# Two graph convolutions of a four-layer GNN kernel: the product with the weights, the scaling by degrees and the split into bf16 parts gathered into one stage

## The chip, the cores and the metric

One core of one Trainium2 chip runs the whole kernel. The metric is the device time of one execution in microseconds (us); the kernel before takes 8021.73 us, the median of three runs.

## What is computed

Four graph layers follow each other, each added to its input and normalised over 64 features. The change touches the last one, two graph convolutions over 6250 nodes:

```python
def _gcn_conv(x, src, dst, W, b):
    h = x @ W
    deg = 1.0 + jax.ops.segment_sum(jnp.ones_like(dst, dtype=h.dtype), dst, num_segments=N)
    dinv = jax.lax.rsqrt(deg)
    norm = dinv[src] * dinv[dst]
    msg = h[src] * norm[:, None]
    agg = jax.ops.segment_sum(msg, dst, num_segments=N)
    return agg + h * (1.0 / deg)[:, None] + b
h = jax.nn.relu(_gcn_conv(x, src, dst, W1, b1))
return _gcn_conv(h, src, dst, W2, b2)
```

There are 200000 edges. `x` is 6250 x 64 and `W` 64 x 64, all f32.

## The kernel before, in words

The nodes stand as 125 partitions by 50 blocks (NL = 125, NB = 50) by 64 features (D). Earlier stages have sorted the edges and made `counts`, a matrix of u8 edge counts between nodes, in tiles of 128 x 128; a row of it is 50 such tiles, 800 KB, loaded as two halves of 400 KB. Edges that found no slot there are "spilled" and handled one by one.

A convolution is two stages, each a block of its own with a rendezvous of all engines at its end.

`project` (line 517, called in lines 2100 and 2102) computes x @ W in f32, two blocks a round, 25 rounds. ScalarE copies a block to a buffer (L539), TensorE transposes ("turns") it (L553), ScalarE copies the turned block out of PSUM (L544), TensorE multiplies it with the weights (L557, which the profile shows as two instructions for one f32 product), VectorE copies the product to `hh` (L565, in the profile `node_sums`). There are two buffers of everything.

`convolve` (line 1990) calls `spread` (from line 1306) with one pass. On VectorE it begins with `before_vector`: `xs = h * dinv` for all 3200 elements of a partition (L1996), then `to_parts` (L1140 to L1143), which splits `xs` into three bf16 parts whose sum is the f32 value: cast, subtract, cast, subtract. A wait for a constant (`spilled.const`) stands ahead. Then come the 50 rows of `counts`. SyncE loads the tiles (L1338, two rows ahead), ScalarE (L1374) and VectorE (L1458) each cast their share of a tile to bf16, TensorE multiplies 50 tiles with the parts (L1395) and adds the node's own row (L1403), VectorE sums the three parts' columns (L1464), and later, two rows at a time, finishes `z` (L2001 to L2009). TensorE handles the first two rows together and finishes both at the end. A row's cast buffer is free again when TensorE has finished the row two before.

The spilled edges run beside. GpSimd clears `y_rows` at the start (L1200). ScalarE, in its queue behind its four first casts and a wait on `posted`, which VectorE raises after `before_vector`, writes `xs` to a table in memory, `rows` (L1193). GpSimd waits for that table, reads the spilled edges (L1208), and gathers their nodes (L1216); after row 5 TensorE compares ids (L1236), VectorE scales the gathered rows (L1269), TensorE sums (L1242), GpSimd adds the result to `y_rows` (L1222) and loads it as `y_sb` (L1227). TensorE and VectorE stand in their queues at this point until that work is through; rows 6 and on come after it.

The stage that opens the whole kernel (`front`) has turns in groups of four blocks (L143) and products with 192 columns (L132), its copies all on VectorE; the sort stage has f32 products of 64 columns (L402). The last layer norm (L1102 to L1111) follows the second convolution.

Of the kernel before, what the change touches and what calls it, by code (L numbers as in the profile page):

```python
# [5 lines left out]
F32, BF16, I32, I16, U8 = mybir.dt.float32, mybir.dt.bfloat16, mybir.dt.int32, mybir.dt.int16, mybir.dt.uint8  # L6
ALU, ACT, AX = mybir.AluOpType, mybir.ActivationFunctionType, mybir.AxisListType

N_NODES, D = 6250, 64
N_EDGES = 200000  # L10
NB = 50
NL = N_NODES // NB
# [499 lines left out]
                dve.tensor_copy(n_spilled[:], pad_f[:, 0:1])  # L512
                dve.tensor_copy(n_pairs[:], pad_f[:, 1:2])

def project(nc, tag, x, weights, out, ident, n_out):

    with ExitStack() as ctx:
        sb = lambda name, shape, dt: ctx.enter_context(nc.sbuf_tensor(f"{tag}_{name}", shape, dt))  # L520
        pb = lambda name, shape: ctx.enter_context(nc.psum_tensor(f"{tag}_{name}", shape, F32))
        sem = ctx.enter_context(Semaphores(nc))
        two = range(2)
        block = [sb(f"block{u}", [NL, D], F32) for u in two]
        block_t = [sb(f"block_t{u}", [D, NL], F32) for u in two]
        ps_t = [pb(f"ps_t{u}", [128, 512]) for u in two]
        ps_o = [pb(f"ps_o{u}", [128, 512]) for u in two]
        taken = sem("taken")

        staged, turned, turned_sb, product, kept = (sem(n) for n in ("staged", "turned", "turned_sb", "product", "kept"))  # L530
        with nc.Block() as blk:
            @blk.scalar
            def _(act):
                act.sem_inc(turned, 2)
                act.sem_inc(product, 2)
                with act.Fori(0, NB // 2) as it:
                    for u in two:
                        act.wait_ge(turned, 2 * it + (u + 1))
                        act.activation(block[u][:], x[:, bass.ds(2 * it + u, 1), :].rearrange("p a d -> p (a d)"),  # L539
                                       ACT.Copy).then_inc(staged, 1)  # L540
                    for u in two:
                        act.wait_ge(turned, 2 * it + (u + 3))
                        act.wait_ge(product, 2 * it + (u + 1))
                        act.activation(block_t[u][:], ps_t[u][0:D, 0:NL], ACT.Copy).then_inc(turned_sb, 1)  # L544

            @blk.tensor
            def _(pe):
                pe.sem_inc(kept, 2)
                with pe.Fori(0, NB // 2) as it:
                    for u in two:  # L550
                        pe.wait_ge(staged, 2 * it + (u + 1))
                        pe.sem_inc(taken, 1)
                        nc.tensor.transpose(ps_t[u][0:D, 0:NL], block[u][:], ident[0:NL, 0:NL]).then_inc(turned, 1)  # L553
                    for u in two:
                        pe.wait_ge(turned_sb, 2 * it + (u + 1))
                        pe.wait_ge(kept, 2 * it + (u + 1))
                        nc.tensor.matmul(ps_o[u][0:NL, 0:n_out], block_t[u][:], weights, start=True,  # L557
                                         stop=True).then_inc(product, 1)

            @blk.vector  # L560
            def _(dve):
                with dve.Fori(0, NB // 2) as it:
                    for u in two:
                        dve.wait_ge(product, 2 * it + (u + 3))
                        dve.tensor_copy(out[:, bass.ds(2 * it + u, 1), :].rearrange("p a d -> p (a d)"),  # L565
                                        ps_o[u][0:NL, 0:n_out]).then_inc(kept, 1)


N_RP = NB // 2
# [568 lines left out]
def to_parts(link, dve, parts, whole, rest):  # L1138

    link(dve.tensor_copy(parts[:, :, 0, :], whole[:]))  # L1140
    link(dve.tensor_tensor(rest[:], whole[:], parts[:, :, 0, :], ALU.subtract))
    link(dve.tensor_copy(parts[:, :, 1, :], rest[:]))
    link(dve.tensor_tensor(parts[:, :, 2, :], rest[:], parts[:, :, 1, :], ALU.subtract))  # L1143


def wide(col):

    return col[:].unsqueeze(2).to_broadcast([NL, NB, D])
# [130 lines left out]
def pair_rows(p):  # L1279
    return slice(2 * p, 2 * p + 2) if isinstance(p, int) else bass.ds(2 * p, 2)  # L1280
# [706 lines left out]
               lambda k: 2 if k == PASSES - 1 else 7, False)  # L1987


def convolve(nc, tag, shared, ident16, h, out, bias, relu, dinv, xs, parts, sums, y_sb, rest, counts):  # L1990

    with ExitStack() as ctx:
        z = ctx.enter_context(nc.sbuf_tensor(f"{tag}_z", [NL, 2, D], F32))

        def before_vector(dve, link):
            link(dve.tensor_tensor(xs[:], h[:], wide(dinv), ALU.mult))  # L1996
            to_parts(link, dve, parts, xs, rest)

        def post(dve, link, k, p):
            b = pair_rows(p)  # L2000
            link(dve.tensor_tensor(z[:], sums[:, b, :], y_sb[:, b, :], ALU.add))  # L2001
            yield
            link(dve.tensor_tensor(z[:], z[:], dinv[:, b].unsqueeze(2).to_broadcast([NL, 2, D]), ALU.mult))
            yield
            link(dve.tensor_tensor(z[:] if relu else out[:, b, :], z[:],
                                   bias[:].unsqueeze(1).to_broadcast([NL, 2, D]), ALU.add))
            yield
            if relu:
                link(dve.tensor_scalar(out[:, b, :], z[:], 0.0, None, ALU.max))  # L2009
                yield  # L2010

        spread(nc, tag, 1, counts, SRC, DST, *shared, ident16, xs, (parts, parts), sums, y_sb, before_vector, post,
               lambda k: 4 if relu else 3, True)


def load_layer3(nc, io, w, bias):
    with ExitStack() as ctx:
        loaded = ctx.enter_context(Semaphores(nc))("w3_loaded")
        with nc.Block() as blk:
            @blk.sync  # L2020
            def _(sp):
                for i in range(2):
                    sp.dma_start(w[i][:], io[f"L3_gnn_W{i + 1}"]).then_inc(loaded, 16)
                    sp.dma_start(bias[i][:], io[f"L3_gnn_b{i + 1}"].rearrange("(a n) -> a n", a=1)
                                 .to_broadcast([NL, D])).then_inc(loaded, 16)
                sp.wait_ge(loaded, 64)


def build(nc, io, out):
# [7 lines left out]
    counts = dram("counts", [NB, 128, NB, 128], U8)  # L2037
    counts_t = dram("counts_t", [NB, 128, NB, 128], U8)
    Semaphores.made = {}
    with ExitStack() as ctx:  # L2040
        sb = lambda name, shape, dt, c=ctx: c.enter_context(nc.sbuf_tensor(name, shape, dt))
        n_spilled = sb("n_spilled", [TE, 1], I32)
        n_pairs = sb("n_pairs", [TE, 1], I32)
        x = sb("x", [NL, NB, D], F32)
        ident = sb("ident", [128, 128], F32)
        ident16 = sb("ident16", [128, 128], BF16)
# [23 lines left out]
        hh = node_sums[:, :, 0:D]  # L2070
        xs, y_sb = [sb(name, [NL, NB, D], F32) for name in ("xs", "y_sb")]

        both = sb("sums_rest", [NL, 2, NB, D], F32)
        sums, rest = both[:, 0], both[:, 1]
        parts2 = both[:].rearrange("p a b d -> p (a b d)").bitcast(BF16)[:, 0:NB * 3 * D]\
            .rearrange("p (b i d) -> p b i d", i=3, d=D)
        parts = sb("parts", [NL, NB, 3, D], BF16)
        dinv1, dis2, dinv3 = (sb(name, [NL, NB], F32) for name in ("dinv1", "dis2", "dinv3"))
        coeff = sb("coeff", [NL, 6], F32)
        w3 = [sb(f"w3_{i}", [D, D], F32) for i in range(2)]  # L2080
        bias3 = [sb(f"bias3_{i}", [NL, D], F32) for i in range(2)]
        rows = dram("rows", [N_NODES, D], F32)
        y_rows = dram("y_rows", [NL * YB, D], F32)
        shared = (io, sorted_rows, rows, y_rows, n_pairs, ident)
# [12 lines left out]
        layer_norm(nc, "ln2", x, hh[:], 1.0, rest)  # L2097

        load_layer3(nc, io, w3, bias3)
        project(nc, "conv1_of", x, w3[0][:], hh, ident, D)  # L2100
        convolve(nc, "conv1", shared, ident16, hh, hh, bias3[0], True, dinv3, xs, parts, sums, y_sb, rest, counts)
        project(nc, "conv2_of", hh, w3[1][:], hh, ident, D)
        convolve(nc, "conv2", shared, ident16, hh, hh, bias3[1], False, dinv3, xs, parts, sums, y_sb, rest, counts)
        layer_norm(nc, "ln3", x, hh[:], 1.0, rest, out_rows=out)


# [24 lines left out]
```

## Time and profile before

| what | value |
|---|---|
| time, median of 3 runs | 8021.73 us (8019.52 to 8025.28) |
| time of the profiled execution | 8040.06 us |
| its span | 8038.4 us |
| TensorE matmul busy | 6943.2 us (86%) |
| VectorE busy | 5984.2 us (74%) |
| ScalarE busy | 4364.3 us (54%) |
| the two projections | 7401 to 7447, 7701 to 7747 us |
| the two stages with the matrix rows | 7448 to 7699, 7747 to 7998 us |
| last layer norm | from 8001 us |

The profile comes from one execution, the times of which lie some 18 us above the median. Busy times are averages over very different stages; what the change touches is read from the timeline of its own stretches. PE is TensorE, PEld its weight loads, DVE VectorE, ACT ScalarE, POOL GpSimd, SP SyncE; a trailing q is the engine's queue issuing a DMA. The number behind x counts the instructions that a row merges, and the bracket tells how long the engine was idle before and what ended that.

### The profile page before, as it was taken

The numbers are of one execution on the slowest core, as the hardware profiler recorded it, in microseconds if no ns is written. First come the engines' busy times: TensorE is split into PE (matmuls) and PEld (weight loads), VectorE is DVE, ScalarE is ACT, GpSimd is POOL, SyncE is SP. The second block draws the span as 40 slices with busy tenths as digits, with TensorE's granted clock in tenths as the row PEclk, the third lists the DMA queues.
The fourth block names the chain that finished last, engine by engine and source line by source line (L and its number), as shares of the span: only waits on it lengthen the run. The fifth ranks groups of instructions, "written<-read, shape, count | busy, mean of one in ns | idle before, by whom it ended". The sixth has DMA issues, their size and how long they took to land. (4 is left out here: it accounts for less than half of the span.)

```text
span 8038.4 us, 279490 instructions
## 1 busy us (share of the span) xinstructions
PE 6943.2 (86%) x98699; PEld 5917.8 (74%) x98724; DVE 5984.2 (74%) x17395; ACT 4364.3 (54%) x13164; POOL 2862.3 (36%) x2957
## 2 busy tenths in 40 slices
PE   2499999999999799999994788888895999998887
PEld 1255555555555499999993787787895988897877
DVE  4367677767776699898995799799898766775556
ACT  0122222222222299999993787787794655665545
POOL 0388888888888755454552000000000000000000
PEclk9999999999999999999996999999998999998878
DMA  7622222322222277676674887787894766664645
GB/s 309 226 59 59 61 59 59 60 60 59 60 60 59 53 233 232 223 233 227 229 231 139 287 298 275 280 300 275 297 334 178 200 197 197 198 195 122 182 132 153
DMA packets 656412, 1425.60 MB, mean 177 GB/s; under 512 B 284336, under 2 KB 351662, under 8 KB 652737
## 3 DMA queue, kind: packets, MB, share of 16 engines
q1 hardware_dynamic: 542402, 1245.12, 48.0%
q0 software_dynamic: 101792, 92.82, 5.5%
q10 hardware_dynamic: 11668, 80.52, 2.5%
q8 instruction: 322, 5.28, 0.3%
q14 instruction: 228, 1.87, 0.1%
HBM read 982.95 MB, written 433.34 MB: 176 GB/s over the span
## 5 line engine op out<-in xcount | busy, mean ns | idle before, releaser
L330 POOL DMA_INDIRECT sorted_rows<-sort_rows,sort_row_at x1600 | 1979.6, 1237 | 579.7 <-issue 566.6
L1593 ACT ACTIVATE smooth_msg<-smooth_ps_a,smooth_w_rows 128x64 f32<-128x64 f32 x6000 | 1312.4, 333 | 335.4 <-PE smooth_ps_a L1679 317.5
L360 ACT ACTIVATE sort_count<-sort_ps_c 50x50 bf16<-50x50 f32 x1600 | 331.7, 207 | 1935.7 <-PE sort_ps_c L392 1935.7
L1374 ACT ACTIVATE poly_cast<-poly_mat 128x1536 bf16<-128x1536 uint8 x500 | 713.9, 1475 | 462.1 <-PE poly_ps L1395 359.0
L388 PEld LDWEIGHTS sort_ps_r<-sort_count,sort_hot_dt 50*125 50x125 bf16 x1600 | 283.0, 177 | 837.3 <-issue 582.8
L402 PE MATMUL sort_ps_m<-sort_w,sort_hidden 128*125 128x64 f32 x3200 | 879.3, 430 | 0.0
L381 PE MATMUL sort_ps_h<-sort_attrs,sort_w 24*128 24x500 f32 x800 | 812.0, 1116 | 45.1 <-DMA sort_attrs<-in_attr_t 45.1
L1701 PE MATMUL smooth_ps_s<-smooth_msg,smooth_hot 128*128 128x64 bf16 x7500 | 771.3, 195 | 82.3 <-DVE smooth_last_part L1832 66.1
L1701 PE MATMUL smooth_ps_s<-smooth_rest,smooth_hot 128*128 128x64 bf16 x7500 | 766.8, 194 | 6.5 <-issue 6.5
L1701 PE MATMUL smooth_ps_s<-smooth_last_part,smooth_hot 128*128 128x64 bf16 x7500 | 765.9, 194 | 6.9 <-issue 6.9
L402 PEld LDWEIGHTS sort_ps_m<-sort_w,sort_hidden 128*125 128x125 f32 x3200 | 732.1, 320 | 41.1
L1701 PEld LDWEIGHTS smooth_ps_s<-smooth_msg,smooth_hot 128*128 128x128 bf16 x7500 | 687.5, 99 | 99.8 <-DVE smooth_last_part L1832 67.9
L741 ACT ACTIVATE graph_hot_t<-graph_ps_t 128x1024 bf16<-128x1024 bf16 x625 | 641.7, 1027 | 126.9 <-PE graph_ps_t L784 96.6
L1701 PEld LDWEIGHTS smooth_ps_s<-smooth_rest,smooth_hot 128*128 128x128 bf16 x7500 | 690.3, 99 | 15.4 <-issue 15.4
L1701 PEld LDWEIGHTS smooth_ps_s<-smooth_last_part,smooth_hot 128*128 128x128 bf16 x7500 | 687.4, 98 | 11.3 <-issue 11.2
L1395 PE MATMUL poly_ps<-parts,poly_cast 125*128 125x192 bf16 x7500 | 643.4, 250 | 55.1 <-DVE poly_cast L1458 24.1
L817 PE MATMUL graph_ps_kv<-kv_parts,graph_hot_t 125*128 125x128 bf16 x7500 | 686.1, 219 | 0.0
L1822 DVE TENSOR_TENSOR smooth_rest<-smooth_msg 128x640 f32<-128x640 f32 x750 | 617.8, 824 | 88.1 <-ACT smooth_msg L1593 34.4
L1395 PEld LDWEIGHTS poly_ps<-parts,poly_cast 125*128 125x128 bf16 x7500 | 633.1, 99 | 65.2 <-issue 28.0
L711 POOL TENSOR_TENSOR graph_parts<-graph_parts 128x260 f32<-128x260 f32 x625 | 387.4, 620 | 745.2 <-DVE graph_hot L873 740.7
L814 PE MATMUL graph_ps_q<-q_parts,graph_hot_t 125*128 (+1 forms) x7500 | 633.0, 193 | 15.5 <-ACT graph_hot_t L741 9.2
L1832 DVE TENSOR_TENSOR smooth_last_part<-smooth_rest 128x640 bf16<-128x640 f32 x750 | 616.0, 821 | 13.8
(332 smaller groups left out, 16537.9 us busy)
## 6 DMA issues: line engine op xcount, KB each, us to landing
poly_mat<-counts_t SPq DMA_DIRECT2D x500, 400.0 KB, 3.7
smooth_src<-src_rows SPq DMA_DIRECT2D x150, 960.0 KB, 5.1
smooth_hot<-hot_rows SPq DMA_DIRECT2D x150, 960.0 KB, 7.0
smooth_src<-src_rows SPq DMA_DIRECT2D x150, 640.0 KB, 5.9
smooth_hot<-hot_rows SPq DMA_DIRECT2D x150, 640.0 KB, 7.0
graph_edges<-sorted_rows SPq DMA_DIRECT2D x125, 700.0 KB
hot_rows<-graph_hot SPq DMA_DIRECT2D x125, 640.0 KB, 3.6
src_rows<-graph_hot_t SPq DMA_DIRECT2D x125, 640.0 KB, 3.5
```

The lines of the kernel that those rows point to most:

```text
L330: pool.indirect_dma_start(out=sorted_rows, out_offset=bass.IndirectOffsetOnAxis(row_at[u][:, j:j + 1], 0), in_=rows[u][:, j, :], in_offset ...
L381: nc.tensor.matmul(ps_h[h][:, 0:H * TE], w1[:], attrs[u][:, h * H * TE:(h + 1) * H * TE], start=True, stop=True).then_inc(hidden_ps, 1)
L402: last = nc.tensor.matmul(ps_m[u][0:TE, t * D:(t + 1) * D], hidden[u][:, t * TE:(t + 1) * TE], w2[:], start=True, stop=True, skip_group_ch ...
L741: act.activation(hot_t[x.b][:, :, :, x.s, :].rearrange("p e t v d -> p e t (v d)"), ps_t[x.g % 2][:].rearrange("p e t v d -> p e t (v d)") ...
L814: nc.tensor.matmul(ps_q[:, 2 * t + v], d_t, q[:, i], start=i == 0, stop=i == 2, skip_group_check=True)
L817: last = nc.tensor.matmul(ps_kv[u][:, 2 * t + v], s_t, kv_parts[:, s, i], start=i == 0, stop=i == 2, skip_group_check=True)
L1374: act.activation(cast[u][h][:, DVE_S:HR, :], mat[u][h][:, DVE_S:HR, :], ACT.Copy)\
L1395: last = nc.tensor.matmul(ps[u][:, 0:3 * D], cast[u][b // HR][0:NL, b % HR, :], parts[k % 2][:, b].rearrange("p i d -> p (i d)"), start=b ...
L1593: last = act.activation(at[:, i, :], ps_a[g % 2][:, i * D:(i + 1) * D], ACT.Copy, scale=w_rows[u][:, c * CHUNK + i:c * CHUNK + i + 1])
L1701: last = nc.tensor.matmul(ps_s[u][:, 0:D], hot[u][t][:, at // 2, :, at % 2], part[:, i, :], start=False, stop=c == N_CHUNKS - 1 and i == C ...
L1822: dve.tensor_tensor(rest[c][:], msg[c][:], high(msg[c]), ALU.subtract).then_inc(firsts, 1)
L1832: dve.tensor_tensor(last_part[c][:], rest[c][:], high(rest[c]), ALU.subtract)\
```

## The change

`project` is gone. A new stage, `conv_rows`, takes a block's rows directly from `x` for the turn, with no copy ahead. It turns four blocks into one PSUM bank and copies them with one ScalarE instruction, multiplies each with the weights into a bank that holds eight blocks, scales eight blocks by `dinv` with one VectorE instruction straight from PSUM into `xs`, and makes the three parts there too, eight blocks at a time: the two casts on ScalarE, the two subtractions on VectorE. TensorE turns group i before it multiplies group i-1. `before_vector` is empty, and `hh` no longer holds the product.

```diff
-def project(nc, tag, x, weights, out, ident, n_out):
...
-def convolve(nc, tag, shared, ident16, h, out, bias, relu, dinv, xs, parts, sums, y_sb, rest, counts):
+def conv_rows(nc, tag, x, w, dinv, xs, parts, left, ident):
...
+            @blk.tensor
+            def _(pe):
+                def products(i):
+                    pe.wait_ge(turned_sb, i + 1)
+                    o = quads[i].start // OCT
+                    if o >= 2 and quads[i].start == octs[o].start:
+                        pe.wait_ge(scaled, o - 1)
+                    for b in range(quads[i].start, quads[i].stop):
+                        at = b - octs[o].start
+                        last = nc.tensor.matmul(ps_o[o % 2][0:NL, at * D:(at + 1) * D],
+                                                xt[i % 2][:, (b - quads[i].start) * NL:(b - quads[i].start + 1) * NL], w,
+                                                start=True, stop=True, skip_group_check=True)
+                    if quads[i].stop == octs[o].stop:
+                        last.then_inc(product, 1)
+
+                for i, q in enumerate(quads):
+                    if i >= 2:
+                        pe.wait_ge(turned_sb, i - 1)
+                    for b in range(q.start, q.stop):
+                        last = nc.tensor.transpose(ps_t[i % 2][0:D, (b - q.start) * NL:(b - q.start + 1) * NL], x[:, b, :],
+                                                   ident[0:NL, 0:NL])
+                    last.then_inc(turned, 1)
+                    if i >= 1:
+                        products(i - 1)
+                products(len(quads) - 1)
+
+            @blk.scalar
+            def _(act):
+                def turn(i):
+
+                    act.wait_ge(turned, i + 1)
+                    act.activation(xt[i % 2][:, 0:size(quads[i]) * NL], ps_t[i % 2][0:D, 0:size(quads[i]) * NL], ACT.Copy)\
+                       .then_inc(turned_sb, 1)
+
+                def first(o):
+                    act.wait_ge(scaled, o + 1)
+                    act.activation(parts[:, octs[o], 0, :], xs[:, octs[o], :], ACT.Copy).then_inc(firsts, 1)
+
+                def second(o):
+                    act.wait_ge(rests, o + 1)
+                    act.activation(parts[:, octs[o], 1, :], left[:, octs[o], :], ACT.Copy).then_inc(seconds, 1)
+
+                n = len(octs)
+                for i in range(n + 3):
+                    for j in (2 * i, 2 * i + 1):
+                        if j < len(quads):
+                            turn(j)
+                    if 0 <= i - 2 < n:
+                        first(i - 2)
+                    if 0 <= i - 3 < n:
+                        second(i - 3)
+
+            @blk.vector
+            def _(dve):
+                def scale(o):
+                    dve.wait_ge(product, o + 1)
+                    s = octs[o]
+                    dve.tensor_tensor(xs[:, s, :], ps_o[o % 2][0:NL, 0:size(s) * D].rearrange("p (b d) -> p b d", d=D),
+                                      dinv[:, s].unsqueeze(2).to_broadcast([NL, size(s), D]), ALU.mult).then_inc(scaled, 1)
+
+                def rest(o):
+                    dve.wait_ge(firsts, o + 1)
+                    dve.tensor_tensor(left[:, octs[o], :], xs[:, octs[o], :], parts[:, octs[o], 0, :], ALU.subtract)\
+                       .then_inc(rests, 1)
+
+                def last_part(o):
+                    dve.wait_ge(seconds, o + 1)
+                    dve.tensor_tensor(parts[:, octs[o], 2, :], left[:, octs[o], :], parts[:, octs[o], 1, :], ALU.subtract)
+
+                n = len(octs)
+                for o in range(n + 2):
+                    if o < n:
+                        scale(o)
+                    if 1 <= o <= n:
+                        rest(o - 1)
+                    if o >= 2:
+                        last_part(o - 2)
+
+
+def convolve(nc, tag, shared, ident16, out, bias, relu, dinv, xs, parts, sums, y_sb, counts):
...
         def before_vector(dve, link):
-            link(dve.tensor_tensor(xs[:], h[:], wide(dinv), ALU.mult))
-            to_parts(link, dve, parts, xs, rest)
+            pass
...
-        project(nc, "conv1_of", x, w3[0][:], hh, ident, D)
...
+        conv_rows(nc, "conv1_of", x, w3[0][:], dinv3, xs, parts, rest, ident)
...
```

With NB = 50 there are 13 groups of four blocks (`quads`, the last of two) and 7 of eight (`octs`, the last of two). The second convolution is changed in the same way.

## Rows read from the trace of the kernel before

**Rows 1.** Busy time by stretch, first projection (columns named in the first line)

```profile
core 0: us, PE busy (x) PEld busy (x) DVE busy (x) ACT busy (x) POOL busy (x), PEclk, DMA share, GB/s
7401.00:7447.00 46.00, 41.38 (x150) 27.31 (x150) 11.11 (x50) 23.09 (x100) 0.00 (x0) 0.50 0.00 0
```

**Rows 2.** Timeline of the first projection: start, length, engine, line, operands

```profile
7401.29 0.45 ACT L539 ACTIVATE conv_of_block<-x 125x64 f32 x2 [11.86 <-ACTq L534]
...
7443.87 1.10 PE L557 MATMUL conv_of_ps_o<-w,conv_of_block_t 64*125 64x64 f32 x4
...
7444.90 0.62 PE L553 MATMUL conv_of_ps_t<-ident,conv_of_block 125*64 125x125 f32 x2
...
7446.92 0.23 DVE L565 COPY node_sums<-conv_of_ps_o 125x64 f32 x1 [0.20 <-PE conv_of_ps_o L557]
```

**Rows 3.** Timeline of the first convolution's entry to its matrix rows

```profile
7448.40 0.27 SPq L1188 DMA_DIRECT2D conv_before<-in_tri  x1
...
7450.30 1.32 POOL L1200 DMA_DIRECT2D y_rows<-conv_zeros  x1 [0.30 <-POOL conv_zeros L1198]
7450.97 3.49 DVE L1996 TENSOR_TENSOR xs<-node_sums,dinv 125x3200 f32<-125x3200 f32 x1 [3.83 <-DMA conv_lane_col<-in_lanes]
7452.98 5.86 ACT L1374 ACTIVATE conv_cast<-conv_mat 128x1536 bf16<-128x1536 uint8 x4 [7.15 <-DMA conv_mat<-counts]
...
7465.33 0.26 ACTq L1193 DMA_DIRECT2D rows<-xs  x1
...
7466.51 10.02 PE L1395 MATMUL conv_ps<-parts,conv_cast 125*128 125x192 bf16 x98 [19.75 <-DVE conv_cast L1458]
```

**Rows 4.** Timeline of the opening stage, four turns and the products after them

```profile
72.37 1.04 PE L143 MATMUL front_ps_t<-ident,x 125*64 125x125 f32 x4
...
73.34 2.92 PE L132 MATMUL front_ps_o<-w_qkv,front_xt 64*125 64x192 f32 x8
```

**Rows 5.** The sort stage: a stretch (columns as rows 1), four f32 instructions in it

```profile
2000.00:2006.00 6.00, 5.41 (x19) 3.10 (x19) 3.83 (x16) 2.22 (x7) 4.78 (x5) 1.00 0.26 62
...
2004.94 1.10 PE L402 MATMUL sort_ps_m<-sort_w,sort_hidden 128*125 128x64 f32 x4
```

**Rows 6.** Groups of instructions of three other sizes (count, busy us, mean ns, idle before)

```profile
L544 ACT ACTIVATE conv_of_block_t<-conv_of_ps_t 64x125 f32<-64x125 f32 x100 | 24.1, 270 | 36.4 <-PE conv_of_ps_t L553 36.4
...
L741 ACT ACTIVATE graph_hot_t<-graph_ps_t 128x1024 bf16<-128x1024 bf16 x625 | 641.7, 1027 | 126.9 <-PE graph_ps_t L784 96.6
...
L1822 DVE TENSOR_TENSOR smooth_rest<-smooth_msg 128x640 f32<-128x640 f32 x750 | 617.8, 824 | 88.1 <-ACT smooth_msg L1593 34.4
```

**Rows 7.** Timeline of the first convolution, from row 1's end past the spilled edges

```profile
7476.62 0.25 PE L1403 MATMUL conv_ps<-parts,ident 125*128 125x192 bf16 x1
...
7482.25 4.23 ACT L1374 ACTIVATE conv_cast<-conv_mat 128x1536 bf16<-128x1536 uint8 x3 [3.64 <-DMA conv_mat<-counts]
...
7482.94 1.19 POOL L1208 DMA_DIRECT2D conv_edges<-sorted_rows  x1 [31.33 <-DMA rows<-xs]
...
7490.67 1.22 POOL L1216 DMA_INDIRECT conv_of_node<-rows,conv_from_at  x1 [0.30 <-issue]
...
7500.22 0.62 PE L1236 MATMUL conv_ps_spill<-ident,conv_edges 125*125 125x125 f32 x4
...
7504.42 0.29 DVE L1269 TENSOR_TENSOR conv_msg<-conv_of_node,conv_edges 125x128 f32<-125x128 f32 x1
...
7505.71 6.93 PE L1395 MATMUL conv_ps<-parts,conv_cast 125*128 125x192 bf16 x50
...
7512.57 4.29 PE L1395 MATMUL conv_ps<-parts,conv_cast 125*128 125x192 bf16 x50
```

**Rows 8.** Transfers: two stretches (columns as rows 1), two issues of 7447:7520

```profile
7458.00:7461.00 3.00, 0.00 (x0) 0.00 (x0) 2.97 (x2) 0.84 (x1) 0.00 (x0) 0.50 0.32 133
...
7467.00:7470.00 3.00, 3.00 (x21) 2.75 (x20) 2.22 (x3) 0.00 (x0) 0.00 (x0) 0.50 0.93 309
...
y_rows<-conv_zeros POOLq DMA_DIRECT2D x1, 1593.8 KB, 18.9
...
conv_of_node<-rows,conv_from_at POOLq DMA_INDIRECT x2, 4.4
```

More of the change, by code:

```diff
@@ L513, in _ @@
                 dve.tensor_copy(n_pairs[:], pad_f[:, 1:2])
-def project(nc, tag, x, weights, out, ident, n_out):
[L519 to L566, printed above, removed]
@@ L1987, in polynomial @@
                lambda k: 2 if k == PASSES - 1 else 7, False)
-def convolve(nc, tag, shared, ident16, h, out, bias, relu, dinv, xs, parts, sums, y_sb, rest, counts):
+def conv_rows(nc, tag, x, w, dinv, xs, parts, left, ident):
+    QUAD, OCT = 4, 8
+    with ExitStack() as ctx:
+        sb = lambda name, shape, dt: ctx.enter_context(nc.sbuf_tensor(f"{tag}_{name}", shape, dt))
+        pb = lambda name, shape: ctx.enter_context(nc.psum_tensor(f"{tag}_{name}", shape, F32))
+        sem = ctx.enter_context(Semaphores(nc))
+        two = range(2)
+        xt = [sb(f"xt{u}", [D, QUAD * NL], F32) for u in two]
+        ps_t = [pb(f"ps_t{u}", [128, 512]) for u in two]
+        ps_o = [pb(f"ps_o{u}", [128, 512]) for u in two]
+        turned, turned_sb, product, scaled, firsts, rests, seconds = (
+            sem(n) for n in ("turned", "turned_sb", "product", "xs_scaled", "firsts", "rests", "seconds"))
+        quads = [slice(b, min(b + QUAD, NB)) for b in range(0, NB, QUAD)]
+        octs = [slice(b, min(b + OCT, NB)) for b in range(0, NB, OCT)]
+        size = lambda s: s.stop - s.start
+        with nc.Block() as blk:
+            @blk.tensor
[65 more added lines that the diff above has]
+                        last_part(o - 2)
@@ L2099, in build @@
         load_layer3(nc, io, w3, bias3)
-        project(nc, "conv1_of", x, w3[0][:], hh, ident, D)
-        convolve(nc, "conv1", shared, ident16, hh, hh, bias3[0], True, dinv3, xs, parts, sums, y_sb, rest, counts)
-        project(nc, "conv2_of", hh, w3[1][:], hh, ident, D)
-        convolve(nc, "conv2", shared, ident16, hh, hh, bias3[1], False, dinv3, xs, parts, sums, y_sb, rest, counts)
+        conv_rows(nc, "conv1_of", x, w3[0][:], dinv3, xs, parts, rest, ident)
+        convolve(nc, "conv1", shared, ident16, hh, bias3[0], True, dinv3, xs, parts, sums, y_sb, counts)
+        conv_rows(nc, "conv2_of", hh, w3[1][:], dinv3, xs, parts, rest, ident)
+        convolve(nc, "conv2", shared, ident16, hh, bias3[1], False, dinv3, xs, parts, sums, y_sb, counts)
         layer_norm(nc, "ln3", x, hh[:], 1.0, rest, out_rows=out)
```

## The prediction

> **What bounds the kernel now.** I read the page's first part (TensorE 86% busy, but that is an average over stages), then the busy time by stretch around the places that the diff touches, then their timelines. Everything changed lies after 7395 us, in two like copies, one for each convolution.
>
> In the projection, 46 us long, TensorE counts as busy for 41.4 us at a granted clock of 0.50 (the 1.2 GHz level), ScalarE for 23 us, VectorE for 11 us [rows 1]; the second projection is its twin. The timeline shows why this busy TensorE is not a full one: 25 rounds of two blocks take the 45.9 us from ScalarE's first copy at 7401.29 to the end of VectorE's last at 7447.15, 1.8 each, and only 1.03 of that passes between the start of two blocks' products (7443.87) and the next turns (7444.90); the rest goes round over ScalarE's copies [rows 2]. It is a chain of handovers, not an engine at its limit.
>
> Then comes a stretch in which TensorE does nothing. The block is entered at 7448.40 (called B). VectorE waits to B+2.57 for a small constant, then scales and splits in five wide instructions until 7465.3, and only then casts its share of the first matrix rows; TensorE starts at 7466.51, B+18.1, though ScalarE has been casting since 7452.98. The table that the spilled edges are gathered from is written behind VectorE's work too, at 7465.33, B+16.9 [rows 3]. All of this lies on the path.
>
> **Part 1, the stage.** Removed per convolution: 100 ScalarE copies, 50 VectorE copies and the five wide VectorE instructions. TensorE keeps its 50 turns and 50 products, in 13 and 7 groups. Added: 13 wide copies and 14 casts on ScalarE, 21 instructions on VectorE. No DMA is added.
>
> TensorE: the opening stage has the same groups of four turns; from the first to the product behind them it is 73.34 - 72.37 = 0.97 us [rows 4]. Two blocks' products (each shows as two instructions) take 7444.90 - 7443.87 = 1.03 us to the next work, and VectorE's copies behind single products come 0.43 us apart (0.23 long, 0.20 idle), so 0.21 for one instruction more: four blocks are 1.03 + 4 x 0.21 = 1.87 [rows 2]. A group of four is 2.84 us; 12 of them and a half one (0.55 + 1.03) make 35.7 us.
>
> Does the clock change that? In the sort stage, at a granted clock of 1.00, four such instructions with 64 columns take 1.10 us, as four do here at 0.50 [rows 2, 5]. So I put nothing down for the clock.
>
> ScalarE: 125 columns take 270 ns, 1024 take 1027 ns [rows 6], so 0.84 ns a column: 0.59 us for a group's turns, 0.60 for a part of eight blocks. Per eight blocks 2.4 us beside TensorE's 5.7: hidden. VectorE: 3200 columns take 3.49 us [rows 3], 640 take 0.82 [rows 6], 1.04 ns each, so 0.69 us for 512 and about 0.29 for the last 128; three of 0.69 are 2.1 us: hidden. At the end the cover is gone: behind the product group before the last, which ends 1.0 us before TensorE does, VectorE's queue holds six instructions of 0.69 and three of 0.29, 5.0 us, plus some 0.4 of handovers. The stage ends at 7401.3 + 35.7 - 1.0 + 0.1 + 5.4 = 7441.5 in place of 7447.15: **gain 5.6 us**. Bounds: all 150 instructions at 0.21 with no cost of switching, 31.5 us, gain 9.8; products at the opening stage's 2.92 a group (192 columns there) [rows 4], 12.5 x 1.05 = 13 us more, a loss of 7.5.
>
> **Part 2, the start of the block.** `before_vector` is empty now. ScalarE's first cast starts at B+4.6 and takes 1.48, VectorE's first can run beside it, so TensorE starts near B+6.1 in place of B+18.1 [rows 3]. What is late next?
>
> Rows 0 and 1 take 10.1 us as before (7466.51 to 7476.62) [rows 3, 7]: B+16.3. With two rows of buffers, row 2 is cast only then: 1.9 us for a cast and its handovers, then 4.3 a row [rows 3, 7], so B+22.5, row 3 B+26.8. Tiles now travel beside two long transfers. The clearing of y_rows alone moves 133 GB/s at a share of 0.32, about 5 of 16 engines [rows 8]. The table lands 17.6 us after its issue (7482.94, when GpSimd reads the edges) and ScalarE waits 3.6 us for a tile that comes at 7482.25 [rows 3, 7]. In the new kernel the table is issued behind ScalarE's four casts, at B+10.5, and lands near B+28.1; with slow tiles until then, row 4 ends near B+31, row 5 near B+36.
>
> After row 5 the spilled edges are due. The second gather is issued 7.7 us after the table's landing and lands 4.4 later [rows 7, 8]: new B+40.2. VectorE's own steps need 4.2 us from TensorE's arrival (7500.22 to 7504.42) [rows 7]: B+40.2. The rows go on 1.3 us later (7505.71) [rows 7]: B+41.5 in place of B+57.3, 15.8 us. 1.8 of it I keep back: TensorE idles before the spill, and behind such an idle the next row took 6.9 us where 4.3 is usual [rows 7]. **Gain 14 us.** Bounds: 16.5 if the table lands in 15 us; 7, below.
>
> **Sum.** 19.6 a convolution, 39 us. Behind the spill nothing differs: same rows, same reload of y_sb, same layer norm. The profiled execution took 8040.06 us (span 8038.4), 18 above the median of 8021.73; the terms are differences, so they come off the median: **7983 us**.
>
> **Rivals.**
> 1. TensorE has no cost of switching: 2 x (9.8 + 14) = 48, 7974; with the table in 15 us 7969. For: both helpers have slack. Against: four turns and the switch take 0.97 us, not 4 x 0.21 [rows 4]. Chance 0.17.
> 2. The clearing and the table share engines. The clearing lands 18.9 us after 7450.30, B+20.8 [rows 3, 8]; today it meets the table for 3 us, then for 10. Sharing puts the table up to 7 or 8 us later, and the spill with it: part 2 gains 7, time 8021.7 - 25 = 7997. For: 0.32 is 5 engines, and the table has the same 125 partitions. Against: when both ran, with tiles, the share was 0.93 [rows 8]. Chance 0.17. The Trainium skill ("DMA: Bandwidth & Descriptors", "Why a DMA increments its semaphore by 16 and not by 1") takes the largest number up to 16 that divides the outer size, 5 for 125, which the 0.32 bears out; by it ScalarE's transfers use the lowest-numbered engines and GpSimd's a run from a moving cursor, so that an overlap hangs on the cursor. The time would be this rival's.
> 3. Lock step, the slower one: ScalarE and VectorE wait in fixed orders. If a part's wait stood before the next turn, TensorE would wait round the ring: per eight blocks 5.7 + 1.2 + 2.1 + 1.2 = 10.2 us, 64 us a stage against my 40.2. 24 worse, 19.6 better: 8030, and 8056 with products at 2.92 a group. It decides once a helper's queue needs over 5.7 us per eight blocks. Against: `first(i-2)` stands behind turns 2i and 2i+1, what it waits for is two groups old. Chance 0.03.
> 4. The casts don't start early (something else holds VectorE or the tiles): 8021.7 - 11 = 8011. Chance 0.04.
> 5. The fuller stage brings TensorE its 2.4 GHz level, and f32 work halves: TensorE 18 us, gain 23 a stage, 2 x (23 + 14): 7948. Against: four instructions take 1.10 us at either level [rows 2, 5]. Chance 0.02. The Trainium skill ("TensorE: Matmul & The Clock Gate", "What's actually happening") has the array at half its clock when cold, and its gaps are columns over clock; the trace does not bear that out for these f32 products.
>
> The forecast has 0.57, its own range 7977 to 7991; with most of rivals 1 and 2 the range is **7970 to 7999**. A measurement of this kernel tells about 0.2%, 16 us, from no change. Faster by more: 0.57 + 0.17 + 0.17 + 0.02 = 0.93; within: 0.05 (rival 4, the milder half of 3); slower: 0.02.
>
> **What would show it.** About 40 us from the first turn to VectorE's end, groups of four turns 2.84 us apart; TensorE's first matrix product at B+6; the table issued at B+10.5; the spill's message product at B+40; the rows after it at B+42. Wrong would be: groups over 3.5 us apart, ScalarE waiting for VectorE inside the stage, or the rows going on later than B+50.

## The result, and the profile after

The changed kernel took 8005.68 us, the median of 13 executions. Twelve of them lie from 7985.19 to 8012.01; the other, a slow one at 8364.18, was left out of the comparison. The kernel before, run beside it, took 8028.91 us (8019.52 to 8038.58). The two medians are 23 us apart; the ratio over the executions that were kept is 0.9966, 95% interval 0.9958 to 0.9974: about 27 us, 0.34% faster, and this is the figure that I use. I had forecast 39 us and 7983. The kernel before ran 7 us above the 8021.73 from which I had counted, so part of the distance to 7983 is that; 12 us of gain are missing all the same.

| us | before | after |
|---|---|---|
| profiled execution, its span | 8038.4 | 7986.8 |
| start of the layer norm ahead of the convolutions | 7371.1 | 7357.2 |
| from there to B, the first convolution's block | 77.3 | 69.8 |
| from B to the second convolution's B | 298.9 | 280.2 |
| from there to the end | 291.1 | 279.7 |

The first line differs by 51.6 us, which is not the change's worth: 14 of it lie ahead of all that the diff touches. In five profiled executions of the two kernels (two of the one, three of the other) that start lies at 7371.1 and 7362.8 us, and at 7357.2, 7359.4 and 7360.1; in the nine profiled variants below, which leave this stretch alone, anywhere from 7359.3 to 7368.7. The last three lines of the table, the **last part** from here on, add up to 667.3 and 629.7; over the five executions they are 667.3 and 663.3 before, 629.7, 635.6 and 629.3 after, means 665.3 and 631.5, **33.8 us** apart. That is what the change can be seen to do in the profiles. The timed 27 lies some 7 below it, and these 7 I can't place. The three profiled executions of the changed kernel took 7988.53, 7996.67 and 7991.07 us; seven of the twelve above took 8004 to 8012, and no profile shows one of those, so what they do otherwise is open.

The page of the changed kernel, its first lines:

```profile
span 7986.8 us, 278076 instructions
## 1 busy us (share of the span) xinstructions
PE 6915.9 (87%) x98699; PEld 5905.6 (74%) x98724; DVE 5887.1 (74%) x17327; ACT 4339.6 (54%) x13018; POOL 2861.7 (36%) x2957
```

Busy time says little of where the time went: TensorE's fell from 6943.2 to 6915.9, VectorE's from 5984.2 to 5887.1.

The stage, by stretch (answers to [rows 1]):

```profile
core 0: us, PE busy (x) PEld busy (x) DVE busy (x) ACT busy (x) POOL busy (x), PEclk, DMA share, GB/s
7386.00:7427.00 41.00, 35.38 (x150) 28.68 (x150) 12.33 (x21) 14.49 (x27) 0.00 (x0) 0.50 0.00 1
```

TensorE is busy from its first turn to its last product without a gap (35.38 us from 7386.76 to 7422.14), and the granted clock is 0.50 throughout, the 1.2 GHz level. Its timeline, and VectorE's tail (answers to [rows 2]):

```profile
7386.76 1.85 PE L1975 MATMUL conv_of_ps_t<-ident,x 125*64 125x125 f32 x8 [33.60 <-PEq L48]
...
7390.40 1.04 PE L1975 MATMUL conv_of_ps_t<-ident,x 125*64 125x125 f32 x4
...
7391.37 1.94 PE L1965 MATMUL conv_of_ps_o<-w,conv_of_xt 64*125 64x64 f32 x8
...
7419.36 2.78 PE L1965 MATMUL conv_of_ps_o<-w,conv_of_xt 64*125 64x64 f32 x12
...
7421.33 0.69 DVE L2013 TENSOR_TENSOR xs<-conv_of_ps_o,dinv 125x512 f32<-125x512 f32 x1 [1.87 <-PE conv_of_ps_o L1965]
...
7424.74 0.89 DVE L2023 TENSOR_TENSOR parts<-sums_rest,parts 125x512 bf16<-125x512 f32 x2
```

Four turns (7390.40), then the products of the group before (7391.37), and the next turns at 7393.24: a group takes 2.84 us. All ScalarE and VectorE work hides behind it until 7421.33. L2013 scales, L2018 subtracts, L2023 makes the last part.

The entry (answers to [rows 3]); B is 7426.93:

```profile
7426.93 0.27 SPq L1136 DMA_DIRECT2D conv_before<-in_tri  x1
...
7428.82 1.32 POOL L1148 DMA_DIRECT2D y_rows<-conv_zeros  x1 [0.30 <-POOL conv_zeros L1146]
7430.80 2.86 ACT L1322 ACTIVATE conv_cast<-conv_mat 128x1536 bf16<-128x1536 uint8 x2 [5.62 <-DMA conv_mat<-counts]
7430.80 2.10 DVE L1406 CAST conv_cast<-conv_mat 128x1664 bf16<-128x1664 uint8 x2 [5.16 <-DMA conv_mat<-counts]
...
7432.34 4.02 PE L1343 MATMUL conv_ps<-parts,conv_cast 125*128 125x192 bf16 x24 [10.20 <-ACT conv_cast L1322]
```

VectorE now casts its share at once, and TensorE starts at B+5.4 in place of B+18.1. ScalarE and GpSimd further on (answers to [rows 7]):

```profile
7434.37 1.48 ACT L1322 ACTIVATE conv_cast<-conv_mat 128x1536 bf16<-128x1536 uint8 x1 [0.71 <-DMA conv_mat<-counts]
7435.39 0.26 ACTq L1141 DMA_DIRECT2D rows<-xs  x1
...
7442.84 2.86 ACT L1322 ACTIVATE conv_cast<-conv_mat 128x1536 bf16<-128x1536 uint8 x2 [5.62 <-PE conv_ps L1351]
7447.14 1.48 ACT L1322 ACTIVATE conv_cast<-conv_mat 128x1536 bf16<-128x1536 uint8 x1 [1.44 <-DMA conv_mat<-counts]
7455.08 4.23 ACT L1322 ACTIVATE conv_cast<-conv_mat 128x1536 bf16<-128x1536 uint8 x3 [6.46 <-DMA conv_mat<-counts]
...
7456.20 1.68 POOL L1156 DMA_DIRECT2D conv_edges<-sorted_rows  x1 [26.07 <-DMA rows<-xs]
...
7464.71 1.22 POOL L1164 DMA_INDIRECT conv_of_node<-rows,conv_from_at  x1 [0.30 <-issue]
...
7469.05 0.62 PE L1184 MATMUL conv_ps_spill<-ident,conv_edges 125*125 125x125 f32 x4
...
7473.24 0.29 DVE L1217 TENSOR_TENSOR conv_msg<-conv_of_node,conv_edges 125x128 f32<-125x128 f32 x1
```

The fifth of these lines is the one that matters: ScalarE idles 6.46 us until 7455.08, B+28.2, and what ends it is a tile of counts, the second of row 3. TensorE stands still before it:

```profile
7452.00:7455.00 3.00, 0.00 (x0) 0.00 (x0) 0.00 (x0) 0.00 (x0) 0.00 (x0) 0.78 0.52 179
```

Here no engine works at all: the kernel waits for a transfer. The transfers issued in 7426 to 7500 (answers to [rows 8]):

```profile
conv_mat<-counts SPq DMA_DIRECT2D x28, 400.0 KB, 4.9
y_rows<-conv_zeros POOLq DMA_DIRECT2D x1, 1593.8 KB, 24.9
```

The clearing of `y_rows` takes 24.9 us from issue to landing, 18.9 before; the table, issued at B+8.5, lands at B+29.3 (7456.20): 20.8 us, 17.6 before.

### The profile page after: what moved, and what is told of

Read it like the earlier page. It is cut to its first block and busy times, and to the rows that moved or that the text cites. A ratio compares the mean times of both kernels' runs of the same rounds, so it can differ in the third digit from the quotient of the medians.

```text
span 7986.8 us, 278076 instructions
## 1 busy us (share of the span) xinstructions
PE 6915.9 (87%) x98699; PEld 5905.6 (74%) x98724; DVE 5887.1 (74%) x17327; ACT 4339.6 (54%) x13018; POOL 2861.7 (36%) x2957
## 3 DMA queue, kind: packets, MB, share of 16 engines
q14 instruction: 229, 1.88, 0.1%
## 5 line engine op out<-in xcount | busy, mean ns | idle before, releaser
L402 PEld LDWEIGHTS sort_ps_m<-sort_w,sort_hidden 128*125 128x125 f32 x3200 | 732.3, 320 | 41.1
```

The source lines that it names most:

```text
L402: last = nc.tensor.matmul(ps_m[u][0:TE, t * D:(t + 1) * D], hidden[u][:, t * TE:(t + 1) * TE], w2[:], start=True, stop=True, skip_group_ch ...
```

## The experiments

All were run beside the kernel before, whose medians in the four sets were 8029.7, 8027.01, 8028.26 (one run) and 8030.56 us. Ratios are to these.

**Both kernels again.** No edit.

> The kernel before, unchanged. Measures what repeats. In the first profile the part from the start of the third layer norm to the end took 667.2 us (8038.4 - 7371.1). Theory A (the change's own part is steady, the untouched stages wander by some 10 us between executions): this part is again within 3 us of 667, and the rest of the span is where executions differ. Theory B (the part itself wanders): it differs by over 5 us. Times against the kernel before: 1.000 within 0.1%.

> The changed kernel, unchanged. In its first profile the last part took 629.7 us, 37.5 less than before, while the times say only 27 less. Theory A (untouched stages wander): the part is again 630 within 3 us. Theory B (the new start of the block has two outcomes, a good and a bad one, of which the first profile shows a good one): it is 640 to 650, and the tiles of rows 2 to 5 land later than B+28.

> The changed kernel once more, so that the three kernels beside it are compared on one chip. Part from the third layer norm to the end 633 us within 4; second tile of row 3 lands at B+24 to B+29; row 49 reduced at B+238.

The first gave 1.0 (0.9991 to 1.0009), the others 0.996 (0.9946 to 0.9973) and 0.9969 (0.9957 to 0.9981). The last part is steady to 4 us before and to 6 us after, less steady than theory A of the first two texts had it and short of the 640 to 650 of theory B. The pitch of a group was 2.84 us in every copy of the stage. The sum of row 49 comes at B+235.7 and B+237.6 (first and second convolution) in the first profile of the changed kernel, B+240.9 and B+238.4 in the next, B+235.9 and B+236.8 in the third: mean B+237.6. Before it is 247.1 and 249.0, 249.2 and 243.1: mean B+247.1. The blocks therefore gain **9.5 us** each. Out of the same marks, from the layer norm to the first B 77.2 went to 69.8 and from row 49 to the second B 51.8 to 44.5: the stage gains **7.4**. Two times 16.9 are 33.8, which is the last part's 33.8.

The mark of row 49 has a noise of its own. From the sum of row 6 to that of row 49 a block takes either about 182 us or about 185, whatever the kernel: 182.7, 185.7, 185.5 and 182.0 before, 182.3, 185.3, 185.4, 185.4, 182.2 and 182.2 after. What decides between the two is open. For small differences the earlier marks are the better ones: row 6 is summed at B+63.2 before (mean of four) and B+53.7 after (mean of six), the message product comes at B+55.5 and B+46.4.

**The groups alone.** The stage keeps the groups of four and eight, but copies the product to `hh`, and `before_vector` scales and splits as before:

```diff
-                    dve.tensor_tensor(xs[:, s, :], ps_o[o % 2]..., dinv..., ALU.mult)
+                    dve.tensor_copy(hh[:, s, :], ps_o[o % 2]...)
...
         def before_vector(dve, link):
-            pass
+            link(dve.tensor_tensor(xs[:], h[:], wide(dinv), ALU.mult))
+            to_parts(link, dve, parts, xs, rest)
```

> Only the grouping: four-block turns and eight-block products, copied by VectorE to the node buffer; scaling and parts stand in the five wide instructions at the block's start again. My theory: the stage ends right behind the last product, 35.7 us after the first turn and 0.4 of copy, about 9.5 us less than before and 5 less than in the changed kernel; the block's start is as before, TensorE at B+18.1, row 6 at B+64. So 2 x 9.5 = 19 us faster than before. Rival (the stage gave everything, the early start only moves the wait): as fast as the whole change, 27 to 38 us.

Ratio 0.9977 (0.9966 to 0.9987), 18.5 us. Its timeline:

```profile
7429.47 1.13 DVE L1997 COPY node_sums<-conv_of_ps_o 125x512 f32<-125x512 f32 x2 [4.57 <-PE conv_of_ps_o L1964]
7431.74 0.26 SPq L1136 DMA_DIRECT2D conv_before<-in_tri  x1
...
7449.34 0.26 ACTq L1141 DMA_DIRECT2D rows<-xs  x1
...
7450.52 2.72 PE L1343 MATMUL conv_ps<-parts,conv_cast 125*128 125x192 bf16 x16 [20.25 <-DVE conv_cast L1406]
```

TensorE starts 18.8 us behind B again. The wide groups give about two thirds of the timed gain alone (26 of 34 us by the last part, 639.0), since here VectorE has no tail. The other half of the change moves the splitting ahead of B, where it costs a tail of 3 us (the stage's gain falls from 10.8, 77.2 - 66.4, to 7.4), to save 13 at the start, of which 8 are left at the message product (B+54.7 here, B+46.4 in the changed kernel).

**Clearing early.** GpSimd clears `y_rows` while the stage runs, not at B:

```diff
+            @blk.gpsimd
+            def _(pool):
+                pool.memset(zeros[:], 0.0).then_inc(filled, 1)
+                pool.wait_ge(filled, 1)
+                pool.dma_start(y_rows..., zeros...).then_inc(cleared, 16)
+                pool.wait_ge(cleared, 16)
```

> The changed kernel with the clearing of y_rows moved from the convolution's start into the stage before it, where no transfer runs. Theory 1 (the clearing and the table write slow each other and the tiles for rows 2 and 3): table lands near B+24 in place of B+29, the second tile of row 3 by B+20 in place of 24 to 28, row 6 goes on 5 to 8 us earlier, the kernel is 10 to 16 us faster than the changed one. Theory 2 (the table alone starves the tiles): under 2 us a convolution.

Ratio 0.9949 (0.9935 to 0.9963), last part 625.2, 6.4 less than the mean of the changed kernel: less than the 10 to 16 of theory 1, more than theory 2 allows. In the first convolution the second tile of row 3 landed at B+25.8 (2 us sooner; its first came at B+23.4, later than before), row 5 was summed at B+38.1 (4 sooner), the message product came at B+42.1 and in the second at B+43.8. GpSimd found the table at B+26.5.

**The table early.** SyncE writes each eight blocks of `xs` to `rows` as soon as they are scaled:

```diff
+            @blk.sync
+            def _(sp):
+                for o, s in enumerate(octs):
+                    sp.wait_ge(scaled, o + 1)
+                    sp.dma_start(rows...[:, s, :], xs[:, s, :]).then_inc(written, 16)
+                sp.wait_ge(written, 16 * len(octs))
```

> The changed kernel with the table written in the stage before, by SyncE, eight blocks at a time as VectorE scales them, and landed before the stage ends; the clearing stays at the start of the block. Theory 1 (each of the two long transfers takes its share of the same engines from the tiles): row 3's second tile lands near B+17, row 5 ends near B+36, some 5 us a convolution gained over the changed kernel, more than the clearing alone brought (3.8), because a table piece is 12.8 KB against 4.4. Theory 2 (whichever transfer is left starves the tiles as much): under 2 us. The stage must not become longer: 35.4 us from TensorE's first turn to its last product.

Ratio 0.9959 (0.9945 to 0.9973), last part 619.6, 11.9 less. Row 5 at B+35.5, the message product at B+39.9 and, in the second convolution, B+41.5, where it waits 1.5 us for the gather: GpSimd is now held by the clearing.

**Both early.**

> Clearing and table both in the stage before. Theory 1: nothing slows the tiles, rows 2 to 5 follow each other at 4.2 us, row 5 ends at B+34, the spill's message product comes 4.2 us later at B+38, row 49 is reduced near B+230: 8 us a convolution less than the changed kernel, 16 in all, about 49 us or 0.6% under the kernel before. Theory 2 (the rate of the tiles themselves is the limit, 190 GB/s): rows still 5 us or more apart, gain under 8 us in all.

Ratio 0.9943 (0.9929 to 0.9956), last part 620.5. TensorE's timeline in the first convolution, B = 7436.81:

```profile
7452.64 0.25 PE L1355 MATMUL conv_ps<-parts,ident 125*128 125x192 bf16 x1
7454.30 4.30 PE L1347 MATMUL conv_ps<-parts,conv_cast 125*128 125x192 bf16 x50 [1.41 <-ACT conv_cast L1325]
...
7458.52 4.29 PE L1347 MATMUL conv_ps<-parts,conv_cast 125*128 125x192 bf16 x50
...
7462.72 4.29 PE L1347 MATMUL conv_ps<-parts,conv_cast 125*128 125x192 bf16 x50
...
7466.93 4.29 PE L1347 MATMUL conv_ps<-parts,conv_cast 125*128 125x192 bf16 x50
...
7471.14 0.62 PE L1186 MATMUL conv_ps_spill<-ident,conv_edges 125*125 125x125 f32 x4
```

and VectorE's end of the chain:

```profile
7475.34 0.29 DVE L1219 TENSOR_TENSOR conv_msg<-conv_of_node,conv_edges 125x128 f32<-125x128 f32 x1
```

With both transfers out of the way rows 2 to 5 follow each other every 4.2 us, the spill starts at B+34.3 and the message product at B+38.5 (7475.34). This is the course that I had forecast for the change itself, and 2 us better. Row 49 comes at B+231.4 and B+230.9, 6.4 sooner than in the changed kernel and 15.9 sooner than before: near the 15.8 that I had worked out before keeping something back. So what is missing of the block's gain lies in those two transfers. Up to row 6, where the 3 us above don't enter, each alone gives a part of it: the sum of row 6 comes 3.1 us sooner with early clearing, 5.3 with the early table and 7.9 with both (means of the two blocks, against B+53.7). Row 49 and the last part show no such order, the early table alone being as good as both (B+230.7, 619.6), since both blocks of this run took 185 us behind row 6 and both of the run before it 182. Writing the table in the stage also makes the stage 1 us longer, in either run: 41.1 and 41.2 us from the first turn to B in place of 40.2. By their times only this run is clear of the changed kernel of the same set (0.9957 to 0.9981); the three early versions can't be told from each other (the intervals overlap).

**The table first.** ScalarE issues the table ahead of its first casts:

```diff
+                    if n_passes > 1:
                     pair(k, 0)
...
                     spilled.write_table(act, xs)
+                    if n_passes == 1:
+                        pair(k, 0)
```

> The changed kernel with the table issued ahead of ScalarE's four first casts in the convolutions (about B+2.7 in place of B+9), clearing unmoved. If the order decides (the table should be out of the way before rows 2 and 3 need their tiles), the first four tiles land 2 to 3 us later, TensorE starts at B+8, the table lands near B+22, and the sum is about even or 2 us better a convolution. If only the bytes decide, row 49 stays at B+238.

Ratio 0.9969 (0.9958 to 0.9981), last part 632.7: no gain, and row 49 stayed at B+238.2 (mean of two), as the text expects if only the bytes decide. The table was issued 6 us sooner, at B+2.7, and GpSimd went on at B+31.9, B being 7429.40:

```profile
7461.29 1.19 POOL L1156 DMA_DIRECT2D conv_edges<-sorted_rows  x1 [28.66 <-DMA y_rows<-conv_zeros]
```

What ended its wait was now the clearing, which took 29.0 us in place of 24.9. The table's own landing can't be read from this line, but the queue that carries it had moved the last of its 130 packets between B+26.6 and B+28.6, against B+26.1 to B+28.1 in the changed kernel. Row 5 came at B+44.8. To start a transfer sooner did not end it sooner, and it made the other one later.

**The clock.** My prediction put nothing down for it. First, 80 bf16 products (128 columns, into a bank that is written anew later) stand ahead of each stage's first turn:

```diff
+                for _ in range(80):
+                    nc.tensor.matmul(ps_o[1][:, 0:128], ident16[:], ident16[:], ...)
```

> The changed kernel with 80 bf16 products of 128 columns ahead of the first turn of each of the two stages (their result is overwritten), to bring TensorE's clock to 1.00 before the f32 work. The changed kernel's stage ran at a granted 0.50 from end to end, though TensorE was busy throughout. Theory 1 (f32 work has the same pace at both levels): at 1.00 a group of four blocks still takes 2.84 us. Theory 2 (the level sets the pace, my rival 5): groups of 1.4 to 2 us as long as 1.00 is granted. Both: the 80 products add 6 to 8 us a stage. Whether the level holds at 1.00 through 35 us of f32 work is open: if it falls, f32 work does not keep it.

One execution: 7991.06 us beside 8028.26. Its timeline in the first stage:

```profile
7398.38 6.17 PE L1972 MATMUL conv_of_ps_o<-ident 128*128 128x128 bf16 x80 [33.70 <-PEq L48]
...
7405.65 1.08 PE L1965 MATMUL conv_of_ps_o<-w,conv_of_xt 64*125 64x64 f32 x8 [0.24 <-ACT conv_of_xt L1990]
7406.66 0.62 PE L1978 MATMUL conv_of_ps_t<-ident,x 125*64 125x125 f32 x4
...
7408.99 1.94 PE L1965 MATMUL conv_of_ps_o<-w,conv_of_xt 64*125 64x64 f32 x8
7410.86 1.04 PE L1978 MATMUL conv_of_ps_t<-ident,x 125*64 125x125 f32 x4
```

and by stretch, the last one in the second stage:

```profile
7402.00:7406.00 4.00, 3.76 (x57) 3.49 (x55) 0.00 (x0) 0.99 (x2) 0.00 (x0) 1.00 0.00 0
7406.00:7410.00 4.00, 4.00 (x28) 3.30 (x28) 0.69 (x1) 1.23 (x3) 0.00 (x0) 0.81 0.00 0
7410.00:7414.00 4.00, 4.00 (x19) 3.31 (x19) 0.20 (x1) 0.58 (x1) 0.00 (x0) 0.50 0.01 4
7692.00:7696.00 4.00, 4.00 (x33) 3.29 (x32) 0.95 (x2) 1.76 (x4) 0.00 (x0) 1.00 0.00 0
```

At a granted 1.00 (2.4 GHz) four turns take 0.62 us and eight product instructions 1.08, at 0.50 1.04 and 1.94: a group is 1.56 us instead of 2.84. In the first stage the level fell back at 7408.5, some 4 us after the first turn (7404.38), in the second it held to the end. The same f32 work, then, follows the clock; it did not bring the clock up by itself (35 us of it at 0.50 above), and here it kept it in one stage of two.

Then the same, with the warming work hidden: 50 such products while the weights are loaded, 50 behind the first convolution's last row, 20 ahead of the first turn; and last, six more behind each group of four:

```diff
+def keep_busy(nc, n, ps, ident16):
+    for _ in range(n):
+        nc.tensor.matmul(ps[:, 0:128], ident16[:], ident16[:], ...)
...
+                    keep_busy(nc, 6, ps_w, ident16)
```

> The changed kernel with bf16 products of 128 columns where TensorE stands idle: 50 while the weights are loaded, 50 after the first convolution's last row, 20 ahead of the first turn of each stage; their results are not used. The last run showed 1.56 us a group of four blocks at a granted 1.00 and 2.84 at 0.50, and a level that held through the second stage but fell after 6 us in the first. Theory 1 (f32 work keeps the level if it starts on it): both stages 1.56 us a group throughout, 20 us of TensorE each, 15 less than the changed kernel, 28 us faster than it in all. Theory 2 (f32 work does not keep it, and the second stage was luck): the level falls within some 6 to 12 us, gain 4 to 10 us a stage.

> As the run before, and six bf16 products behind each group of four blocks (0.33 us a group at 1.00). Theory 1: no better than without them, 13 x 0.33 = 4 us a stage slower. Theory 2: the level now holds at 1.00 through both stages, 1.9 us a group, 24 us of TensorE a stage, 11 less than the changed kernel, 22 us faster in all, and steadier than without them.

Hidden: 0.9957 (0.9944 to 0.9971), not to be told from the changed kernel by its times (0.9966, in another set), though its profile shows 1.56 us a group in both stages and a last part of 606.9. Its five executions lie from 7974.56, the one with the profile, to 8005.29; that the level held in some and fell in others would explain it, but is not shown. Kept: 0.9935 (0.9922 to 0.9949), executions from 7971.94 to 7981.56, last part 611.9. A group of the last version, from its timeline:

```profile
7407.59 0.59 PE L1984 MATMUL conv_of_ps_t<-ident,x 125*64 125x125 f32 x4
7408.11 1.08 PE L1973 MATMUL conv_of_ps_o<-w,conv_of_xt 64*125 64x64 f32 x8
7409.12 0.51 PE L1942 MATMUL conv_of_ps_w<-ident 128*128 128x128 bf16 x6
7409.47 0.59 PE L1984 MATMUL conv_of_ps_t<-ident,x 125*64 125x125 f32 x4
```

A group takes 1.88 us (7407.59 to 7409.47), in both stages all through: 0.3 dearer than the bare 1.56, 1.0 cheaper than 2.84. From the first turn to B it is 28.5 us in place of 40.2.

**Everything together.** Both transfers early, and the level kept.

> Clearing and table in the stage before, and TensorE kept at its level as in the run before this. The two gains add: stages of 24 us and rows 2 to 5 without a stall, about 22 + 16 us under the changed kernel, 0.8 to 0.9% under the kernel before. Rival: the table's pieces of the last blocks now land after the shorter stage, or ScalarE and VectorE become its bound; then it gives 10 us less.

7959.24 us (7955.41 to 7966.97), ratio **0.9913** (0.99 to 0.9927), last part 601.3: 71 us under the kernel before, over twice the change's own gain. Both causes are there: from the first turn to B each stage takes 29.5 us, 11.7 less than with both transfers early and no level kept, and the message product comes at B+39.4 and B+38.1.

## Why the prediction was wrong

The direction and the two mechanisms were right, the size was not: 39 forecast, 27 timed, 34 read from the profiles. Per convolution the stage gave 7.4 us where I had 5.6, and the block 9.5 where I had 14. By the prediction's own steps:

- **TensorE in the stage, 35.7 us.** Right: 35.4 (7386.76 to 7422.14), a group at exactly 2.84.
- **VectorE's tail, 5.4.** 4.3 us (7421.33 to 7425.63). I had added durations of 0.69, but such instructions, where none waits for the one before, start 0.60 apart (7421.33, 7421.94, 7422.54). The first turn also came 0.6 us sooner, without ScalarE's copy ahead. The term was mis-sized: stage 7.4 in place of 5.6.
- **"TensorE starts near B+6.1".** Right: B+5.4 and B+5.9. So was row 1, forecast to end at B+16.3: TensorE ended it at B+16.0 (7442.97).
- **"Row 3 B+26.8 ... row 4 ends near B+31, row 5 near B+36".** This is the step that failed. I had seen that tiles would travel beside two long transfers, but charged that only to rows 4 and 5, a few us in all. The tiles ran short in row 3 already, its second tile landing at B+28.2; row 3 was summed at B+33.9 and row 5 at B+42.3. With the two transfers out of the way the same sums came at B+26.1 and B+34.5.
- **"New B+40.2".** I had the gather and the row chain arrive at once. The gather was less late than the rows: its second half was issued at B+37.8 (7464.71) and takes 4.8, so it was there at B+42.6, while TensorE came to the spill at B+42.1 (7469.05) and VectorE's 4.2 us put the message product at B+46.3, directly behind its other instructions with no wait. The **row chain** set the spill. 6.1 us later than forecast takes 15.8 to 9.7, and 9.5 was measured; the 1.8 that I kept back for the row behind the spill was not needed.
- **"I put nothing down for the clock."** The number was right and its reason wrong. I took 1.10 us for four f32 instructions at a column of 1.00 [rows 5] as proof that the pace doesn't follow the clock. The runs above show that it does. The 1.00 of [rows 5] can't have been granted: the opening stage's four turns, under a 1.00 too, take 1.04 [rows 4], the pace that the same turns have at 0.50 here (7390.40), while at a real 1.00 they take 0.62. My own rows held the contradiction: four f32 instructions of 125 columns take 0.62 in [rows 7] (7500.22), where the column reads 1.00 late in the trace, and 1.04 in [rows 4]. In the trace of the kernel before, the column reads 1.00 in every stretch up to 3.33 ms, even where TensorE does nothing for 30 us:

```profile
2770.00:2800.00 30.00, 0.00 (x0) 0.00 (x0) 0.63 (x1) 0.00 (x0) 16.96 (x15) 1.00 0.15 30
```

Later in the same trace it is seen to move: TensorE stands still for 4 us ahead of 7504.82, and the column is at 0.50 from 7505 to 7506. It seems to be filled in until the first record of the clock; that is my reading, not something a run settles.

Of the rivals, no switching cost (1) is out: a group at 2.84 holds the 0.97 that I had measured. The shared transfers (2) came nearest, 7997 and a gain of 25 us. That is close to the timed 27 in part by luck: its block gave 7 where 9.5 was measured, its stage 5.6 where it was 7.4, and it counts from 8021.73. It was right that both become slower where they overlap, clearing by 6 us and table by 3, but its price, a table 7 or 8 us late that holds up the gather, was not what was paid; the tiles paid. The Trainium skill ("DMA: Bandwidth & Descriptors", "Why a DMA increments its semaphore by 16 and not by 1") spreads a 128-partition tile over 16 engines and one of 125 over 5. That fits what is seen: a tile needs the busy engines too, and is as late as the slowest of them. That is an argument from the page; no run here shows single engines at it. Lock step (3) and late casts (4) did not happen. The clock (5) was wrong for this kernel, which stays at 0.50, and right in its rule, which I had given 0.02 for the wrong reason: a kernel that is given the level does the stage in 28.5 us.

## What to carry to other kernels

When a change brings the start of a stage forward, its transfers meet others that they used to follow: price the smallest, most frequent transfer under that overlap first, since it feeds the engine, and move a bulk transfer into the stage before, where the queues are empty. A durable check on a reading that "two levels of the clock give the same duration": find the same instruction form at both levels within the stretch in which the clock is recorded, where the column is seen to move. A busy engine is not a fast one; f32 work filled TensorE to the last us at half its clock.

## What the runs showed of the hardware that I had not expected

- 35 us of gapless f32 turns and products (64 to 125 columns) stayed at a granted 0.50, in all six copies of the changed kernel's stage that have a profile; 80 bf16 products of 128 columns, 6.17 us, brought 1.00. The Trainium skill ("TensorE: Matmul & The Clock Gate", "What's actually happening") has the clock released by how busy the engine has been; by that I would have expected the level in this stage, and the trace does not agree.
- Started at 1.00, the same work kept the level in three of four profiled stages and lost it some 4 us after the first turn in the fourth. Why is open. With six bf16 products in each group it held in all four stages that were profiled, which is too few to show that they are needed; the narrower spread of the times (10 us in place of 31) speaks for it.
- Independent VectorE instructions of 0.69 us start 0.60 us apart, so a sum of durations is too long by an eighth. In the layer norm, where each waits for the one before, they start just behind its end (7371.12, 3.49 us long, next at 7374.65 in the kernel before).
- The table issued 6 us sooner was through its queue no sooner (B+26.6 to B+28.6 against B+26.1 to B+28.1), and the clearing beside it took 29.0 us in place of 24.9.
